# GPS layer on one core: destination search and id fetches of the front, laid beside the projection

## The reference

```python
xn = _layernorm(x, axis=-1)
x = x + _L0_gnn_ref(xn, edge_index, edge_weight1, Wq, bq, Wk, bk, Wv, bv, Wo, bo) + _L0_mix_ref(xn[None], ...)[0]
x = x + _L0_ffn_ref(_layernorm(x, axis=-1)[None], ...)[0]
# _L0_gnn_ref, r = source and c = destination of an edge:
q, k, v = (feats @ Wq.T + bq), (feats @ Wk.T + bk), (feats @ Wv.T + bv)      # 8 heads of 32
sim = einsum('hed,hed->eh', q[:, c], k[:, r]) * scale
attn = softmax of sim over the edges of one destination
agg = segment_sum(attn * v[:, r], c)
return agg @ Wo.T + bo
```

## Time and profile before

| what | value |
|---|---|
| median of 3 runs | 2956.17 us (2955.47 to 2956.94) |
| the profiled execution's own time | 2953.88 us |
| its span in the profile | 2952.6 us |
| mean granted TensorE clock, share of full speed | 0.875 |
| busy: PE, DVE, ACT, POOL | 2191.0, 2449.9, 1078.0, 1974.0 us |
| HBM read and written | 512.54 MB, 69.78 MB |

### The profile page before, as it was taken

One profiled execution on the slowest core, in us unless ns is written; L12 is line 12 of the kernel. 1 busy time (PEld: TensorE's weight loads), 2 busy tenths in 40 slices (PEclk: granted clock), 3 DMA queues, 4 the chain that ended last, 5 costly groups with the idle time before them and its releaser, 6 DMA issues. The chain is left out here.

```text
span 2952.6 us, 37856 instructions
## 1 busy us (share of the span) xinstructions
PE 2191.0 (74%) x9653; PEld 1727.9 (59%) x9654; DVE 2449.9 (83%) x3309; ACT 1078.0 (37%) x4488; POOL 1974.0 (67%) x1979
## 2 busy tenths in 40 slices
PE   5753777787766777887877767777885655599998
PEld 4551555455555665665666545555664435499988
DVE  5763878888888899999999888899999987566765
ACT  2300211112366666666666411111111114256463
POOL 4175777777777777777777777777777727335453
PEclk9975887888899899989999878999898875599999
DMA  8517888888877777777777788888887735423341
GB/s 249 182 43 156 238 238 239 241 244 247 230 217 218 218 218 218 220 217 218 218 220 217 226 233 248 249 253 253 252 246 223 210 121 171 117 69 82 82 92 15
DMA packets 262373, 579.18 MB, mean 196 GB/s; under 512 B 57174, under 2 KB 141582, under 8 KB 262136
## 3 DMA queue, kind: packets, MB, share of 16 engines
q0 software_dynamic: 151392, 469.80, 57.6%
q1 hardware_dynamic: 101606, 99.38, 10.7%
q10 hardware_dynamic: 9296, 9.05, 0.9%
HBM read 512.54 MB, written 69.78 MB: 197 GB/s over the span
## 5 line engine op out<-in xcount | busy, mean ns | idle before, releaser
L1128 POOL DMA_INDIRECT wide<-kv_d,arena x1099 | 1053.8, 959 | 334.8 <-issue 326.9
L1463 PE MATMUL ps<-wide,arena 128*128 128x264 f32 x2432 | 699.0, 450 | 176.5 <-DVE wide L1566 176.4
L1463 PEld LDWEIGHTS ps<-wide,arena 128*128 128x128 f32 x2432 | 534.4, 225 | 329.4 <-DVE wide L1566 216.7
L1128 POOL DMA_INDIRECT arena<-kv_d,arena x539 | 516.3, 958 | 164.2 <-issue 160.6
L1255 ACT ACTIVATE ps<-wide 128x256 f32 x229 | 88.8, 388 | 1259.0 <-DVE arena L1532 1255.0
L1535 DVE TENSOR_REDUCE arena<-arena 128x64 f32<-128x2048 f32 x229 | 523.4, 2286 | 7.9
L1532 DVE TENSOR_TENSOR arena<-wide,ps 128x2048 f32<-128x2048 f32 x153 | 349.4, 2284 | 114.1 <-DMA wide<-kv_d,arena 113.8
L1463 PE MATMUL ps<-arena 128*128 128x264 f32 x1216 | 338.1, 439 | 88.7 <-DVE arena L1566 88.5
L140 PE MATMUL ps<-halves 128*128 128x256 f32 (+2 forms) x2304 | 360.7, 318 | 2.0 <-DVE halves L1801 2.0
L1566 DVE TENSOR_TENSOR wide<-wide,ps 128x2112 f32<-128x2112 f32 x152 | 356.7, 2347 | 0.0
L1463 PEld LDWEIGHTS ps<-arena 128*128 128x128 f32 x1216 | 259.5, 218 | 160.8 <-DVE arena L1566 108.9
(11 more groups left out here) (348 smaller groups left out, 3255.2 us busy)
## 6 DMA issues: line engine op xcount, KB each, us to landing
wide<-kv_d,arena POOLq DMA_INDIRECT x1099, 3.8
arena<-in_w SPq DMA_DIRECT2D x16, 1024.0 KB, 5.7
kv_d<-wide SPq DMA_DIRECT2D x49, 260.0 KB, 2.4
arena<-xt_d SPq DMA_DIRECT2D x82, 128.0 KB, 3.5
arena<-kv_d,arena POOLq DMA_INDIRECT x539, 3.8
h_d<-wide SPq DMA_DIRECT2D x7, 903.0 KB, 5.1
row_d<-wide SPq DMA_DIRECT2D x7, 896.0 KB, 9.1
xs_d<-wide SPq DMA_DIRECT2D x49, 128.0 KB, 3.6
```

The lines of the kernel that those rows point to most:

```text
L1128: e.indirect_dma_start(out=kvb[k][:, j, :], out_offset=None, in_=kv_d, in_offset=bass.IndirectOffsetOnAxis(ap=ixb[k][:, j:j + 1], axis=0)) ...
L1463: m = e.matmul(psE[(k + 1) % 3][:, 0:264], ident, kvb[b][:, j, 256:ROW], start=(j == 0), stop=(j == J - 1))
```

## The change

- The first destinations are read from the input `dst` and not from the padded copy: three small DMAs at the head of SP's queue, with no wait for the copy.
- On VectorE the statistics of the first group of x move behind the one-hots of the histogram, and its centering behind the count and the row numbers `blk`.
- `ranks` begins before the projection loop. Each quarter of the dst rows has a semaphore of its own; PACE gives the yields ahead of each quarter's compare, and compare and sum stand in one step. The second pump per tile begins at t = 19 (WAIT_ROWS = 18) instead of 41.
- The ids are fetched in four parts with a semaphore each (OWN), and `pump` has SP store a part at the steps OWN_STEPS, counted from the fetch.
- The 13 table fetches no longer wait for the end of the loop: they are placed where the last group's statistics have been stored to `row_d` (t = 43), and wait for the last part of the ids. One matmul of the tables writes PSUM bank 3 instead of 6, which the loop uses.

```diff
@@ -31,7 +31,10 @@
-WAIT_ROWS = 40
+WAIT_ROWS = 18
+PACE = (3, 6, 5, 5)
+OWN = ((0, 16), (16, 32), (32, 41), (41, 49))
+OWN_STEPS = (17, 31, 39, 46)
@@ -196,6 +199,16 @@
+        firsts = temp(13)
+        fi_i = temp(13).bitcast(i32)
+        s_fi = sem("s_fi")
+        assert 12 * 128 < NB - 1 < 13 * 128 and (NB - 1) * 128 < E
+        dma(Y, fi_i[:, 0:12], dst[0:12 * 128 * 128].rearrange("(a p j) -> p a j", p=128, j=128)[:, :, 0], s_fi, allow_slow_non_contiguous=True)
+        wait(Y, v(V.memset(fi_i[:, 12:13], 1 << 20)))
+        dma(Y, fi_i[0:NB - 1 - 12 * 128, 12:13], dst[12 * 128 * 128:(NB - 1) * 128].rearrange("(p j) -> p j", j=128)[:, 0:1], s_fi,
+            allow_slow_non_contiguous=True)
+        t_fi = dma(Y, fi_i[NB - 1 - 12 * 128:NB - 12 * 128, 12:13], dst[(NB - 1) * 128:(NB - 1) * 128 + 1].rearrange("(p j) -> p j", j=1), s_fi)
@@ -266,11 +279,6 @@
-        firsts = temp(13)
-        fi_i = temp(13).bitcast(i32)
-        wait(Y, t_ed)
-        t_fi = dma(Y, fi_i, dst_d.rearrange("(a p) j -> p a j", p=128)[:, :, 0], s_fi, allow_slow_non_contiguous=True)
@@ -320,16 +328,6 @@
-        wait(V, t_x[0])
-        spread(xbuf[0], range(7))
-        t_nm = {0: offsets(0, root(0))}
-        wait(V, t_nm[0])
-        for i in range(7):
-            t_n0 = v(V.tensor_scalar(out=cen[:, i, :], in0=xbuf[0][:, i, :], scalar1=stat[:, 0, i, 0:1], scalar2=stat[:, 0, i, 1:2],
-                                     op0=ALU.mult, op1=ALU.add))
-        t_n = {(0, 6): t_n0}
@@ -359,6 +357,9 @@
         t_hist = sp.inc(m)
+        wait(V, t_x[0])
+        spread(xbuf[0], range(7))
+        t_r0 = root(0)
         t = v(V.memset(cnt[:, 0:1], 0.0))
@@ -373,6 +374,16 @@
         blki = temp(50).bitcast(i32)
+        wait(V, t_cnt)
+        t = v(V.tensor_scalar(out=blk, in0=cnt, scalar1=-1.0, scalar2=0.0, op0=ALU.add, op1=ALU.max))
+        wait(V, t)
+        t_blk = v(V.tensor_copy(blki, blk))
+        t_nm = {0: offsets(0, t_r0)}
+        wait(V, t_nm[0])
+        for i in range(7):
+            t_n0 = v(V.tensor_scalar(out=cen[:, i, :], in0=xbuf[0][:, i, :], scalar1=stat[:, 0, i, 0:1], scalar2=stat[:, 0, i, 1:2],
+                                     op0=ALU.mult, op1=ALU.add))
+        t_n = {(0, 6): t_n0}
         rows = R1[:, 2 * NBP:2 * NBP + 6400].bitcast(i32).rearrange("p (t j) -> p t j", j=128)
@@ -386,55 +397,58 @@
         rest = R1[:, 10596:10646]
-        s_row = sem("s_row")
+        s_row = [sem(f"s_row{i}") for i in range(4)]
         QUARTERS = [(0, 13), (13, 26), (26, 39), (39, 50)]
-        more = [None]
+        more, steps, t_own, t_ids = [None], [], [None] * 4, [None] * 4
...
                     more[0] = None
+                if steps:
+                    steps[0] += 1
+                    if steps[0] in OWN_STEPS and None in t_ids:
+                        store_own()
...
             wait(G, t_blk, t_ed)
-            for c in range(50):
-                s_row.inc(G.indirect_dma_start(out=rows[:, c, :], out_offset=None, in_=dst_d,
-                                               in_offset=bass.IndirectOffsetOnAxis(ap=blki[:, c:c + 1], axis=0)), 16)
+            for q, (c0, c1) in enumerate(QUARTERS):
+                for c in range(c0, c1):
+                    s_row[q].inc(G.indirect_dma_start(out=rows[:, c, :], out_offset=None, in_=dst_d,
+                                                      in_offset=bass.IndirectOffsetOnAxis(ap=blki[:, c:c + 1], axis=0)), 16)
...
             wait(G, t_rp, t_src)
-            for c in range(NT):
-                t_own = s_ix.inc(G.indirect_dma_start(out=own[c // 32][:, c % 32, :], out_offset=None, in_=src_d,
-                                                      in_offset=bass.IndirectOffsetOnAxis(ap=rpc[:, c:c + 1], axis=1)), 16)
-            return t_own
...
-        def store_own(t_own):
-            wait(Y, t_own)
-            ids_of = row_d.rearrange("(p c) d -> p c d", c=NT)
-            dma(Y, ids_of[:, 0:32, 256:320], own[0].bitcast(f32), s_own)
-            return dma(Y, ids_of[:, 32:NT, 256:320], own[1].bitcast(f32), s_own)
+            for i, (c0, c1) in enumerate(OWN):
+                for c in range(c0, c1):
+                    t_own[i] = s_ix[i].inc(G.indirect_dma_start(out=own[c // 32][:, c % 32, :], out_offset=None, in_=src_d,
+                                                                in_offset=bass.IndirectOffsetOnAxis(ap=rpc[:, c:c + 1], axis=1)), 16)
...
+        def store_own():
...
+            i = t_ids.index(None)
+            c0, c1 = OWN[i]
+            wait(Y, t_own[i])
+            t_ids[i] = dma(Y, row_d.rearrange("(p c) d -> p c d", c=NT)[:, c0:c1, 256:320],
+                           own[c0 // 32][:, c0 % 32:c0 % 32 + c1 - c0, :].bitcast(f32), s_own)
...
         def ranks():
-            wait(V, t_cnt)
-            t = v(V.tensor_scalar(out=blk, in0=cnt, scalar1=-1.0, scalar2=0.0, op0=ALU.add, op1=ALU.max))
-            wait(V, t)
-            take_rows(v(V.tensor_copy(blki, blk)))
-            for _ in range(WAIT_ROWS):
-                yield
-            wait(V, (s_row, s_row.n))
-            for c0, c1 in QUARTERS:
+            take_rows(t_blk)
+            for q, (c0, c1) in enumerate(QUARTERS):
+                for _ in range(PACE[q]):
+                    yield
+                wait(V, (s_row[q], s_row[q].n))
                 t = v(V.tensor_tensor(less[:, c0:c1, :], rows[:, c0:c1, :],
                                       nodeid[:, c0:c1].unsqueeze(2).to_broadcast([128, c1 - c0, 128]), ALU.is_lt))
-                yield
                 wait(V, t)
                 t = v(V.tensor_reduce(fine[:, c0:c1], less[:, c0:c1, :], AX.X, ALU.add))
-                yield
             wait(V, t)
...
             t = v(V.tensor_copy(rpc[:, 0:NT], rp[:, 0:NT]))
-            t_own = take_own(t)
+            take_own(t)
+            steps.append(0)
             wait(V, t)
@@ -544,15 +558,15 @@
-            yield from tables(found[3], r3(sorted_[:, 0:3 * NT], NT), t_own)
+            yield from tables(found[3], r3(sorted_[:, 0:3 * NT], NT))
...
-        s_ix, s_own = sem("s_ix"), sem("s_own")
+        s_ix, s_own = [sem(f"s_ix{i}") for i in range(4)], sem("s_own")
...
-        projected, t_rn, t_xr, t_q49 = [], {}, {}, [None]
+        t_rn, t_xr, t_q49 = {}, {}, [None]
@@ -575,12 +589,12 @@
             t_ds = v(V.tensor_copy(permS[:, 0:NT], fx))
-            while not projected:
+            while 6 not in t_rn:
                 yield
-            t_ids = store_own(t_own)
-            wait(V, t_ids)
+            while None in t_ids:
+                store_own()
             t_q49[0] = v(V.memset(qi[:, NT, :], 0.0))
-            wait(G, t_q49[0], t_ds, t_xr[6], t_ids, t_rn[6])
+            wait(G, t_q49[0], t_ds, t_xr[6], t_ids[3], t_rn[6])
             for c in range(FIRST_Q):
@@ -633,7 +647,7 @@
-                made_.append(sp.inc(T.matmul(ps[5 + i][0:1, 0:CH], cf[:, i:i + 1], ind[0:50, :], start=True, stop=True)))
+                made_.append(sp.inc(T.matmul(ps[(5, 3, 7)[i]][0:1, 0:CH], cf[:, i:i + 1], ind[0:50, :], start=True, stop=True)))
...
@@ -734,6 +748,8 @@
+        more[0] = ranks()
+        pump()
         for grp in range(7):
@@ -779,8 +795,6 @@
-                    if u == 0:
-                        more[0] = ranks()
@@ -791,7 +805,6 @@
-        projected.append(True)
```

More of the change, by code:

```diff
@@ L250, in gps_layer_kernel @@
         t_x[1] = load_x(1, S)
-        s_pad, s_ed, s_fi = sem("s_pad"), sem("s_ed"), sem("s_fi")
+        s_ed = sem("s_ed")
         zero = R3[:, 2048:2176]
@@ L565, in gps_layer_kernel, with tables @@
         t_rg = [None]
-        def tables(t_tb, digit, t_own):
+        def tables(t_tb, digit):
             v(V.memset(R3[0:1, 3848:3848 + TW * (CH + 2) // 2], 0.0))
@@ L649, in tables @@
             v(V.tensor_scalar(out=nrow, in0=nrow, scalar1=0.0, scalar2=8.0, op0=ALU.max, op1=ALU.min))
-            t = v(V.scalar_tensor_tensor(out=spot, in0=nth[0:1, :], scalar=8.0, in1=ps[6][0:1, 0:CH], op0=ALU.mult, op1=ALU.add))
+            t = v(V.scalar_tensor_tensor(out=spot, in0=nth[0:1, :], scalar=8.0, in1=ps[3][0:1, 0:CH], op0=ALU.mult, op1=ALU.add))
             wait(V, t)
```

## The result

The changed kernel takes **2932.53 us**, the median of 3 runs (2931.70 to 2936.87), against 2956.17 before: a ratio of 0.9924, 95% interval 0.9901 to 0.9946, so 23.6 us less. The profiled execution is the longest of the three, 2936.87 with a span of 2935.6 us, at a mean granted TensorE clock of 0.872.

What follows compares the result with a forecast made beforehand. GpSimd's unbroken train of ring fetches was taken as the bound, so its first fetch sets the end: 232.4 against 265.0, -33 us. Profiled 2953.9 - 33 = 2921, plus 2.3 for the median: 2923 us, range 2902 to 2940.

Steps and rivals of the forecast that it cites:

- the ring's start: First of 1638 attention fetches on GpSimd (L1128): from 265.0 to 232.4, -33 us, moving the program's end by as much.
- First destinations: Three small loads heading SyncE's queue: landed at 8.1, GpSimd's row fetches starting at 17.5 in place of 28.1, ±2.
- The first wait: VectorE at tile 3, waiting for the first quarter's fetched rows: 5.5 us, with hardly any wait at the other quarters.
- What compares do to fetches: GpSimd row fetches beside VectorE's quarter compares: 1.2 us longer for each of three, 3.5 us in all.
- Id fetches: 49 source-id fetches on GpSimd: start at 90 instead of 149.5, end at 155 to 163, stores costing nothing.
- Ranks beside the projection: Rank steps among tiles 19 to 40: start table at 114, 14 steps in 32 us with PE setting the pace.
- T43: Tile 43 of the projection, where row_d's last row group is stored: forecast at 199.
- Rival 1: Projection and rank work dovetail, filling tile idle time better: -48 to -58 us, 2898 to 2908; 17%.
- Rivals 2 and 3: Low TensorE clock in the mixed stretch: for a third, -8 to -18 us, 12%; from tile 19 on, +30, 4%.
- From T43 to the ring: Store landing 9.1 us, then table fetches 23.5, ending at 232; tiles, tables and weights ending at 230; ring at 232.4.
- The table fetches: 13 GpSimd fetches of table rows: from 208.6, taking 23.5 us beside mask and weights, ending at 232.
- The ring is the old one, shifted: After its first fetch the ring runs as before, an unbroken train of 1.26 us per fetch, some 2100 us.

Runs made afterwards that it cites:

- pace_two: `tables_late` with later row compares (WAIT_ROWS = 21, PACE = (6, 6, 6, 4)): 2910.59 us, ratio 0.9831.
- ids_last2: `tables_late` with all four id stores held until behind the projection and VectorE waiting for them ahead of the tables: 2936.10 us, ratio 0.9942.
- mask_index: The changed kernel with the mask behind the last bias step and the xs_d stores behind the ring's index loads: 2921.14 us, ratio 0.9896.
- tables_late: The changed kernel with table fetches, tables and mask waiting again for the end of the projection: 2917.15 us, ratio 0.9884.
- changed_again: The changed kernel itself run once more, on another set's chip and rounds: 2934.88 us, ratio 0.9919.
- the five runs above: The changed kernel, `changed_again`, `mask_last`, `mask_index`, and the changed kernel with only the xs_d stores behind the index loads (2924.76 us).
- mask_last: The changed kernel with one more yield, putting the mask behind the last tile's bias step: 2924.76 us, ratio 0.9910.
- best2: `pace_two` with table fetches at tile 43, weights ahead of the mask, and index loads ahead of the xs_d stores: 2911.07 us, ratio 0.9834.

## Why the prediction was right, and where it was not

The time, the range and the sign held; the path by which the ring's start was to come did not. By its steps:

- *First destinations.* DVE's conversion of them stands at 6.96 (8.1 in the text), row fetches start at 16.11 (17.5). A good 1 us too late throughout, within the ±2.
- *The first wait.* 5.5 us at tile 3: 5.80. But VectorE waits at the second quarter too, 4.35 us where I had "hardly". The step at fault is the tile's price there: the six tiles between the two compares take 13.4 us (38.4 to 51.8), where 2.7 each had been taken, and 13 fetches take 16.3. The pacing of `pace_two` takes 7.1 us of such waits away and brings 9.6 us of start: they are paid in full, and something beside them is gained that no run parts.
- *What compares do to fetches.* The 50 fetches took 65.5 us from the first start to the last, against 49 x 1.257 = 61.6 bare: 3.9 where I took 3.5. The three compares hold 3.1 of it (fetches of 1.49, 2.38 and 2.03 us in place of 0.95); 0.8 lies in the first three fetches, ahead of any compare. (The row that I took 1.2 from, gives 2.32 - 0.96 = 1.4.) I had weighed this against the Trainium skill, "SBUF — State Buffer", section "Who interferes with whom", which infers that descriptor writing is not held up by such a step, and had read that as no cost at all. The same section says that a VectorE step with two SBUF inputs contends with a GpSimd instruction that reads SBUF, and these fetches read their row numbers there (`arena` in the row). So the traces show that the fetch is held up, and not by which of the two.
- *Id fetches* from 90: 89.78. They end at 161.5 (155 to 163). Their stores cost nothing that shows (`ids_last2`).
- *Ranks beside the projection.* Start table 111.0 (114), row_d's last group stored at 193.0 (**T43** = 199). From 89.8 on, the stretch to the start table took 21.2 us (24), the rank steps 31.5 (32), the one-hots 12.3 (11) and the rest up to T43 38.2 (42). Rival 1 would have needed 174. Rivals 2 and 3 asked for a low clock in the rank steps; it was 1.00 from 111 to 142.5. It did fall behind them, to 0.50 from 150 to 160, where VectorE was busy 9.0 us of 10 and set the pace.
- *From T43 to the ring.* This is the step that failed: "table fetches ... 232", with its other end at 230, and "first ring fetch at 232.4". From the last group's store to the ring I had 33.4 us (199 to 232.4), and it took 51.8 (193.0 to 244.8). Two terms make up the 18.4. The first is that last tiles, tables and weights took 39.5 us (193.0 to 232.5) where I had 31: 8.5. Here the clock fell to 0.51. The second is that the ring started 12.3 us behind the weights, where I had 2.4: 9.9. The sum had no term for SyncE's queue. I had read the ring's start as the latest of table fetches and L799, because in the earlier trace rows they end there, and did not ask which of the queues that the mask was moved past held something for the ring. `mask_index` gives back 10.5.
- *The table fetches* were not the bound at all. I had them start at 208.6 and take 23.5 us, drawn out by the mask and L799. They started at 200.6 and took 16.3, since the mask (224.5) and the weights came only after their end at 216.8.
- *Luck.* T43 came 6 us early and hid a third of the miss. With T43 at 199 and the same 51.8 us behind it the ring would have started near 251 and the median would lie near 2938.5, by my estimate, just inside the range's end of 2940. And the 20.2 us by which the ring did move lie at the very edge of the 20 to 48 that the forecast gave.
- *The last part of the change.* `tables_late`, which takes it away, is 13.5 us earlier: it costs 13.5 of the 33.7 us that the rest gains, 10.5 by what it stands ahead of and 3.0 by the mixture.
- *The ring is the old one, shifted.* Right: no new wait, 2116.4 us of train against 2114.1, and 2110 to 2115 in all other variants. The start moved by 20.2 us and the median by 23.6; the profiled spans differ by 17.0, with 2.3 us lost in the train. `changed_again`, against the kernel before on its own chip, is 21.3 us under it by the medians.

By the first ring fetch the variants split the whole: 265.0 before; 261.1 with the first destinations alone; 251.3 with the search and the ranks beside the projection too; 231.3 with the ids in parts; 244.8 with tables and mask beside the last tiles. So 3.9, 9.8 and 19.9 us of gain, and 13.5 of loss. The ids in parts, together with VectorE's wait for them, are the largest piece.

What stays open: why a tile mixed with tables takes up to 9 us. The hops between VectorE and PE, the waits behind tiles and the halved clock are all in the trace. Of the clock the five runs above show about 2 us over the whole stretch (29.2 against 27.0 at 0.52 and 0.75), though not why the same program got either; the other two no run parts. A tables chain shorter than its 12 to 13 us is what the next gain would need; it was not tried.

## What to carry to other kernels

When a step moves past others, list every queue it passes and, for each, who waits on what stands behind; a start that equals the end of two things may have a third just under them. Judge its room by when it has run to its end and not by when it goes out: here the index loads went out 8 us ahead of the end of the weights, and would have let the ring start only about 1 us before it did. Work that hops between engines in short dependent steps may be poor filler for a pipeline: the tables beside the last tiles saved nothing and cost 3.0 us, while the rank steps, which also hop but keep PE full, took 31.5 us where 32 were forecast. And a wait for data at a fixed place in an engine's queue was paid in full here, where that engine set the pace: place it where the data is there, even if the work behind it starts a little later.

## What the runs showed of the hardware

A GpSimd fetch beside a large VectorE step with both inputs in SBUF stretches as far as that step. The kernel before has it under its mask (L687, L693) and its weights (L799); GpSimd in order of time:

```profile
254.42 6.12 POOL L585 DMA_INDIRECT wide<-row_d,arena  x1 [0.30 <-issue]
260.85 2.61 POOL L585 DMA_INDIRECT wide<-row_d,arena  x1 [0.30 <-issue]
```

And so has every variant whose table fetches meet the mask (three table fetches of `pace_two`, then the VectorE steps of the same stretch, in order of time):

```profile
211.16 6.11 POOL L599 DMA_INDIRECT wide<-row_d,arena  x1 [0.30 <-issue]
217.57 2.61 POOL L599 DMA_INDIRECT wide<-row_d,arena  x1 [0.30 <-issue]
220.49 0.96 POOL L599 DMA_INDIRECT wide<-row_d,arena  x1 [0.30 <-PEq L821]
```

```profile
212.00 3.67 DVE L701 TENSOR_TENSOR arena<-arena 128x3200 bf16<-128x3200 f32 x1
...
216.05 1.10 DVE L707 TENSOR_SCALAR arena<-arena 128x3600 bf16<-128x3600 bf16 x1
217.07 2.29 DVE L813 TENSOR_TENSOR arena<-wide,arena 128x2048 f32<-128x2048 f32 x1
```

The first of the three spans both L701 and L707 and takes 6.11 us in place of 0.96, the second lies beside L813 and takes 2.61. There is a pattern in the ends. A fetch that began under such a step ended 0.82 to 0.83 us behind that step's end: 37.27 behind 36.44, 58.83 behind 58.00 and 75.01 behind 74.18 (the compares of the changed kernel), 159.99 behind 159.17 (L536 there), 220.18 behind 219.36 (L813 in `pace_two`), 153.10 behind 152.27 (L451 in the kernel before). So the price of a compare is not one number: it is what is left of the compare when the fetch begins, less about 0.1. Beside the sums (L444), which read one tensor, it stays at 0.95. In `best2` the 13 fetches were over before the mask, and none took more than 1.15. The granted clock of TensorE, too, followed the work in front of it: 1.00 from 200 to 208 in `tables_late`, with tiles alone and PE busy 6.7 of the 8 us, and 0.52 in the same 8 us of the changed kernel, with PE busy 5.5 of them. But `mask_last` got 0.76 there with the same instructions and PE busy 5.4: two executions of one order of work can get different clocks.
